# Attended sums of two units on three engines, a bias through the first layer, and an interleaved split

## The chip, the cores and the metric

The kernel runs on one core of one Trainium2 chip. The metric is the device time of one execution in microseconds, taken as the median of several runs. The core's engines are TensorE (PE in the profile), VectorE (DVE), ScalarE (ACT), GpSimd (POOL) and SyncE (SP), which here issues most of the loads. Each engine takes its own instructions in program order; semaphores order them between engines.

## What is computed

For 512 users, each with a history of 200 items of 128 features, the kernel computes attention over the history and a three-layer MLP on top. Cut to what matters (E = A = 64):

```
cand = candidate_features @ Wi + bi                  # 512 x 64
hist = history_features @ Wi + bi                    # 512 x 200 x 64
hidden = relu((cand @ Wq)[:, None, :] + hist @ Wk)
scores = where(seq < length, hidden @ Wv, -1e9)      # 512 x 200
attn = softmax(scores, axis=1)
interest = einsum('bs,bse->be', attn, hist)
avg = sum(hist * mask, axis=1) / length
x = concatenate([interest, cand, avg], axis=1)       # 512 x 192
x = relu(bn1(x @ W1 + b1)); x = relu(bn2(x @ W2 + b2)); x = relu(bn3(x @ W3 + b3))
return sigmoid(x @ Wo + bo)[:, 0]
```

`bn(x) = (x - m) / sqrt(v + eps) * g + be`.

## The kernel before, in words

**Tiling.** The users are cut in two halves of 256, which lie on partitions 0 to 63 and 64 to 127. Four users of each half are a unit (two quads of two users, 400 columns each), so there are 64 units; four units are a superblock, of which there are 16. A "pair" is one column of the tables for the MLP: one user of each half. Part 0 of the MLP takes the pairs of units 0 to 57 (232), part 1 the last 24.

**Stages of a unit.** SyncE loads 0.8 MB of history (`load`, six slots). TensorE projects it by `Wi` into `hist_ps` (`project`, L396, two passes of float32). VectorE masks it into `kept` with a running sum for the average (`masked_sum`, L539). TensorE makes the keys in `key_ps` (`keys`, L411), for the unit before. ScalarE adds the query and takes the relu (`relu`, L306). Once a superblock TensorE makes the scores (`score`, L422), VectorE the maximum (`maximum`, L561), ScalarE the exponent (`exponent`, L314), VectorE the inverse of its sum (`invert`, L567). GpSimd then normalises the weights and splits them in three bfloat16 terms (`split`, L259 to L271: `attn`, `part_a`, `rest`, `part_b`, `parts`). TensorE spreads a row of the weights over partitions (`spread_attn`, L441) for the unit seven before (`DELAY = 7`), and VectorE multiplies by `kept` and sums (`attended_sum`, L552), four instructions a unit. The history's sum lacks the bias of `Wi`, so `mean` adds it (L572, L575), and `store_interest` adds it to the attended sums (L581).

**Order.** TensorE's loop over the units is: project the first quad, project the second, scores at every fourth unit from unit 5 on, keys of the unit before, and from unit 7 on the spread of the unit seven before. The first spread waits for `parts(0)`. Warm-up matmuls on zeros (L366) stand at the start: 8, then 6, then 4 between the two quads of unit 0.

**GpSimd's queue.** Masks 0 and 1, the count, then the scale and shift of the three normalisations (L279 to L289, after the late parameters have landed), then for each superblock `split(j)` and `mask(j + 2)`. The last split is VectorE's (L626 to L635).

**The tail.** After the loop TensorE has: scores of the last superblock in two halves, keys of unit 63, the spreads of units 57, 58 and 59, stages 0 and 1 of MLP part 0, six warm-ups, the spreads of units 60 and 61, stage 2, spread 62, stage 3, spread 63, stages 0 of part 1 and 4 of part 0, then stages 1 to 4 of part 1. Stage 1 adds the interest's product to z1, which ScalarE turns into x1 (L322); x2 and x3 follow (L326, L330), and the sigmoid (L334). ScalarE loads the sigmoid's table by a one-element ACTIVATE (L354) after the last exponent. Odd units from 57 on have their spread in `key_ps`, even ones in `attn_ps`.

Of the kernel before, what the change touches and what calls it, by code (L numbers as in the profile page):

```python
# [8 lines left out]
ALU = mybir.AluOpType  # L9
ACT = mybir.ActivationFunctionType  # L10
# [21 lines left out]
DELAY = 7  # L32

SCORE_AT = SB_UNITS + 1

WARMUPS = 8
MORE_WARMUPS = 6
GAP_WARMUPS = 4
TAIL_WARMUPS = 6
COPIES = 3  # L40
# [3 lines left out]

PART_UNITS = UNITS - 6
MLP_PARTS = (slice(0, UNIT_PAIRS * PART_UNITS), slice(UNIT_PAIRS * PART_UNITS, HALF))

# [11 lines left out]
def build(nc, hist_dram, cand_dram, params_dram, lens_dram, out_dram):  # L59
    with ExitStack() as ctx:  # L60
# [49 lines left out]
        attended = sb("attended", [128, HALF])  # L110
        interest = sb("interest", [128, HALF])
        average = sb("average", [128, HALF])
# [60 lines left out]
        attn_spread = sem("attn_spread")  # L173
        attn_summed = sem("attn_summed")
        bn_steps = sem("bn_steps")
        bn_ready = sem("bn_ready")
# [3 lines left out]
        average_ready = sem("average_ready")  # L180
        interest_ready = sem("interest_ready")
        z1_ready = sem("z1_ready")
# [8 lines left out]

        block = ctx.enter_context(nc.Block())

        def wait(eng, semaphore, value):
# [25 lines left out]
        def _(pool):  # L220
# [60 lines left out]
            pool.tensor_tensor(bn_shift[:, :], param("b"), param("m"), ALU.subtract).then_inc(bn_steps, 1)  # L281
            pool.wait_ge(bn_steps, 3)
            pool.tensor_tensor(bn_scale[:, :], bn_scale[:, :], bn_power[:, :], ALU.pow).then_inc(bn_steps, 1)
            pool.wait_ge(bn_steps, 4)
            pool.tensor_tensor(bn_scale[:, :], bn_scale[:, :], param("g"), ALU.mult).then_inc(bn_steps, 1)
            pool.wait_ge(bn_steps, 5)
            pool.tensor_tensor(bn_shift[:, :], bn_shift[:, :], bn_scale[:, :], ALU.mult).then_inc(bn_steps, 1)
            pool.wait_ge(bn_steps, 6)
            pool.tensor_tensor(bn_shift[:, :], bn_shift[:, :], param("be"), ALU.add).then_inc(bn_ready, 1)  # L289

            for j in range(LAST):
                split(j)
                if j + 2 <= LAST:
                    mask(j + 2)

        @block.scalar
        def _(act):
# [39 lines left out]
            act.dma_start(params[:, 0:EARLY], params_dram[:, 0:EARLY]).then_inc(early_landed, 16)  # L337
            act.dma_start(lens_raw[:, :], lens_dram).then_inc(lens_landed, 16)
            act.wait_ge(bias_product, 1)
            act.activation(query_bias[:, :], attn_ps[:, 1, 0:1], ACT.Copy).then_inc(bias_ready, 1)  # L340
# [6 lines left out]
            for unit in range(UNITS):  # L347
                j, at = divmod(unit + 1 - SCORE_AT, SB_UNITS)
                if at == 0 and j >= 0:
                    exponent(j)  # L350
                relu(unit)
            exponent(LAST)

            act.activation(table_loader[:, :], param("bo", slice(0, 1)), ACT.Sigmoid)  # L354
            for stage in range(1, 4):
                mlp_stage(0, stage)
            mlp_stage(1, 1)
            mlp_stage(1, 2)
            mlp_stage(0, 4)
            mlp_stage(1, 3)  # L360
# [3 lines left out]
        def _(pe):  # L364
# [62 lines left out]
            def spread_attn(unit):  # L427
# [4 lines left out]
                if unit == FREE_AT:  # L432
                    pe.wait_ge(relu_done, 4 * (UNITS - 1))
                else:
                    wait(pe, attn_summed, UNIT_PAIRS * (unit - 1 if unit > FREE_AT else unit))
                banks = attn_banks(unit)
# [9 lines left out]
            def mlp_stage(n, stage):  # L446
# [9 lines left out]
                if stage == 1:  # L456
                    pe.wait_ge(interest_ready, n + 1)
                    for h in range(2):
                        rows = slice(64 * h, 64 * h + 64)
                        product = pe.matmul(z1[:, h, pairs], w1[rows, 0, :], interest[rows, pairs],  # L460
                                            start=False, stop=True, skip_group_check=True)
                    product.then_inc(z1_ready, 1)
# [22 lines left out]
            for unit in range(UNITS):  # L485
# [5 lines left out]
                if unit == 0:  # L491
                    queries()
                j, at = divmod(unit - SCORE_AT, SB_UNITS)
                if at == 0 and j >= 0:
# [6 lines left out]
                if unit >= DELAY:  # L501
                    if unit == DELAY:
                        pe.wait_ge(spread_made, 1)
                        pe.wait_ge(query_ready, 1)
                    spread_attn(unit - DELAY)

# [11 lines left out]
            for _ in range(TAIL_WARMUPS):  # L518
                keep_busy((LAST + 1) % 2)
            spread_attn(first + 3)  # L520
            spread_attn(first + 4)
            mlp_stage(0, 2)
            spread_attn(first + 5)
            mlp_stage(0, 3)
            spread_attn(first + 6)
            mlp_stage(1, 0)
            mlp_stage(0, 4)
            for stage in range(1, 5):
# [3 lines left out]
        def _(dve):  # L532
# [9 lines left out]

            def attended_sum(unit, pairs=range(UNIT_PAIRS)):
                dve.wait_ge(attn_spread, unit + 1)
                banks = attn_banks(unit)
                for c in pairs:
                    at, v = divmod(c, 2)
                    q = 2 * unit + at
                    col = UNIT_PAIRS * unit + c

                    wait(dve, attn_summed, col - 3)
                    dve.tensor_tensor_reduce(scratch[:, at, v, :], banks[:, at, v * SEQ:(v + 1) * SEQ], kept[:, q % KEPT_SLOTS, v, :],  # L552
                                             1.0, 0.0, ALU.mult, ALU.add, attended[:, col:col + 1]).then_inc(attn_summed, 1)
# [15 lines left out]
            def mean(n):  # L569
# [6 lines left out]
                                  ALU.mult).then_inc(average_ready, 1)  # L576

            def store_interest(n):
                pairs = MLP_PARTS[n]
                dve.wait_ge(attn_summed, pairs.stop)  # L580
                dve.tensor_scalar(interest[:, pairs], attended[:, pairs], param("bi"), None,  # L581
                                  ALU.add).then_inc(interest_ready, 1)

# [8 lines left out]
            for unit in range(UNITS):  # L592
# [12 lines left out]
                if unit == PART_UNITS + 2:  # L605
# [4 lines left out]

            first = UNITS - DELAY
            attended_sum(first)
            store_interest(0)
            mean(1)
            attended_sum(first + 1)
            maximum(LAST)
            attended_sum(first + 2)
            invert(LAST)
# [7 lines left out]
            dve.tensor_scalar(part_a[:, :], weights[:, bank, :], inverse, param("keep1"),  # L626
                              ALU.mult, ALU.mult).then_inc(split_steps, 1)
            dve.wait_ge(split_steps, done + 1)
            dve.scalar_tensor_tensor(out=rest[:, :], in0=weights[:, bank, :], scalar=inverse, in1=part_a[:, :],
# [6 lines left out]
            for unit in range(first + 3, UNITS):  # L636
                attended_sum(unit)
            store_interest(1)

# [60 lines left out]
```

## Time and profile before

| | |
|---|---|
| median of 3 runs | 212.09 us (210.8 to 212.43) |
| the profiled execution | 211.71 us |
| its span, first to last instruction | 209.7 us |
| TensorE (matmuls) busy | 200.9 us, 96% |
| VectorE busy | 176.8 us, 84% |
| ScalarE busy | 103.5 us, 49% |
| GpSimd busy | 62.6 us, 30% |
| mean granted clock of TensorE | 0.984 |

The busy shares are means over the span. Matmuls are pipelined and their ends are modelled, so a busy TensorE is not one at its peak. The granted clock is a share of the full 2.4 GHz. In timeline rows the second number is how long the group of instructions was busy from its start; consecutive groups of one engine can overlap a little.

### The profile page before, as it was taken

The numbers are of one execution on the slowest core, as the hardware profiler recorded it, in microseconds if no ns is written. First come the engines' busy times: TensorE is split into PE (matmuls) and PEld (weight loads), VectorE is DVE, ScalarE is ACT, GpSimd is POOL, SyncE is SP. The second block draws the span as 40 slices with busy tenths as digits, with TensorE's granted clock in tenths as the row PEclk, the third lists the DMA queues.
The fourth block names the chain that finished last, engine by engine and source line by source line (L and its number), as shares of the span: only waits on it lengthen the run. The fifth ranks groups of instructions, "written<-read, shape, count | busy, mean of one in ns | idle before, by whom it ended". The sixth has DMA issues, their size and how long they took to land.

```text
span 209.7 us, 6308 instructions
## 1 busy us (share of the span) xinstructions
PE 200.9 (96%) x2126; PEld 83.6 (40%) x2126; DVE 176.8 (84%) x1086; ACT 103.5 (49%) x302; POOL 62.6 (30%) x112
## 2 busy tenths in 40 slices
PE   7999999999999999999999999999999999997793
PEld 3422434343434434343434343343444343433422
DVE  1458578989989898989899898989898998998890
ACT  2145355545465553555453655535554536556523
POOL 7903330606051321406060513224060605131000
PEclk9999999999999999999999999999999999999985
DMA  6999999797979797987969797978879793000000
GB/s 201 398 426 416 412 419 391 245 328 249 323 245 322 237 320 266 309 307 269 321 242 300 268 323 237 316 262 317 303 253 326 238 318 130 0 0 5 3 0 0
DMA packets 10225, 53.72 MB, mean 256 GB/s; under 512 B 1105, under 2 KB 2001, under 8 KB 10194
## 3 DMA queue, kind: packets, MB, share of 16 engines
q1 hardware_dynamic: 9906, 52.95, 70.7%
q10 hardware_dynamic: 288, 0.37, 0.6%
q8 instruction: 17, 0.28, 0.5%
q14 instruction: 14, 0.11, 0.1%
HBM read 53.32 MB, written 0.00 MB: 254 GB/s over the span
## 4 chain that ended last, share of the span: by engine, by line
PE 87%; DVE 8%; ACT 2%; issue 2%; DVEq 0%; ACTq 0%
PE hist_ps L396 42%; PE key_ps L411 24%; PE score_ps L422 10%; PE attn_ps L441 5%; DVE scratch L552 3%; DVE kept L539 3%; PE score_ps L366 2%; PE score_ps L473 1%; PE score_ps L465 1%; ACT hidden L306 1%; ACT x L326 1%; PE score_ps L468 0%; PE hist_ps L411 0%; ACT result L334 0%; DVE attended L552 0%
## 5 line engine op out<-in xcount | busy, mean ns | idle before, releaser
L306 ACT ACTIVATE hidden<-key_ps,query 128x200 f32<-128x200 f32 x252 | 86.8, 427 | 54.3 <-PE key_ps L411 54.3
L396 PE MATMUL hist_ps<-history,params 128*64 128x400 f32 x512 | 100.3, 512 | 0.0
L539 DVE SCALAR_TENSOR_TENSOR kept<-item,lens,hist_ps 128x200 f32<-128x200 f32 x256 | 92.7, 419 | 7.2 <-PE hist_ps L396 7.2
L552 DVE CUSTOM_DVE_ANT_0 scratch<-attn_ps,kept 128x200 f32<-128x200 f32 x240 | 73.3, 363 | 9.2 <-PE attn_ps L441 9.2
L411 PE MATMUL key_ps<-kept,params 64*64 64x400 f32 x504 | 57.0, 521 | 0.9 <-ACT hidden L306 0.4
L396 PEld LDWEIGHTS hist_ps<-history,params 128*64 128x64 f32 x512 | 31.2, 136 | 37.1 <-issue 28.4
L259 POOL TENSOR_SCALAR attn<-weights,inv_sum 128x200 f32<-128x200 f32 x15 | 6.5, 435 | 112.6 <-DVE inv_sum L567 112.6
L411 PEld LDWEIGHTS key_ps<-kept,params 64*64 64x64 f32 x504 | 13.6, 131 | 35.9 <-issue 26.7
L422 PE MATMUL score_ps<-hidden,wv_rows 128*32 128x200 f32 x512 | 25.3, 336 | 1.2 <-ACT hidden L306 1.2
L441 PEld LDWEIGHTS attn_ps<-parts,spread 64*64 64x64 bf16 x480 | 15.7, 107 | 24.5 <-issue 19.0
L314 ACT ACTIVATE weights<-scores,neg_max 128x200 f32<-128x200 f32 x16 | 7.4, 462 | 35.5 <-DVE neg_max L561 35.5
L441 PE MATMUL attn_ps<-parts,spread 64*64 64x200 bf16 x480 | 21.5, 246 | 1.7 <-DVE parts L635 1.5
L552 DVE DVE_READ_ACCUMULATOR2_ANT attended<- 128x1 f32 x256 | 21.6, 84 | 0.0
L539 DVE DVE_READ_ACCUMULATOR kept<-item,lens,hist_ps 128x1 f32 x256 | 21.6, 84 | 0.0
L422 PEld LDWEIGHTS score_ps<-hidden,wv_rows 128*32 128x32 f32 x512 | 15.0, 109 | 14.7 <-ACT hidden L306 10.1
L251 POOL TENSOR_SCALAR mask_bias<-item,lens 128x200 f32<-128x200 f32 x16 | 15.4, 961 | 1.5
L561 DVE CUSTOM_DVE_ANT_0 scores<-score_ps,mask_bias 128x200 f32<-128x200 f32 x16 | 5.9, 366 | 4.9 <-PE score_ps L422 4.9
L264 POOL TENSOR_TENSOR rest<-attn,part_a 128x200 f32<-128x200 f32 x15 | 8.5, 569 | 1.3
L271 POOL TENSOR_TENSOR parts<-rest,part_b 128x200 bf16<-128x200 f32 x15 | 8.5, 566 | 1.3
L261 POOL TENSOR_SCALAR part_a<-weights,inv_sum,params 128x200 bf16<-128x200 f32 x15 | 7.6, 507 | 0.0
L366 PE MATMUL score_ps<-warmup 128*128 128x400 bf16 x24 | 6.4, 417 | 1.1 <-DVE warmup L584 1.1
L266 POOL TENSOR_SCALAR part_b<-rest,params 128x200 bf16<-128x200 f32 x15 | 6.5, 434 | 1.5
(69 smaller groups left out, 59.0 us busy)
## 6 DMA issues: line engine op xcount, KB each, us to landing
history<-history_dram SPq DMA_DIRECT2D x63, 800.0 KB, 5.0
history<-history_dram SPq DMA_DIRECT2D x2, 400.0 KB, 4.7
candT<-candidates_dram SPq DMA_DIRECT2D x1, 256.0 KB, 5.5
params<-parameters_dram SPq DMA_DIRECT2D x1, 248.5 KB, 12.1
params<-parameters_dram ACTq DMA_DIRECT2D x1, 226.5 KB, 2.4
lens_raw<-lengths_dram ACTq DMA_DIRECT2D x1, 136.0 KB, 3.8
probability<-result SPq DMA_DIRECT2D x1, 2.0 KB
```

The source lines that it names most:

```text
L251: pool.tensor_scalar(mask_bias[:, j % 2, :], item[:, :], row_len[:, j:j + 1], MASKED, ALU.is_ge, ALU.mult).then_inc(mask_ready, 1)
L261: pool.tensor_scalar(part_a[:, :], weights[:, bank, :], inv_sum[:, bank:bank + 1], param("keep1"), ALU.mult, ALU.mult).then_inc(split_step ...
L264: pool.tensor_tensor(rest[:, :], attn[:, :], part_a[:, :], ALU.subtract).then_inc(split_steps, 1)
L271: pool.tensor_tensor(parts[:, bank, :], rest[:, :], part_b[:, :], ALU.subtract).then_inc(parts_ready, 1)
L306: act.activation(hidden[:, g % HID_SLOTS, v, :], banks[:, v, at * SEQ:(at + 1) * SEQ], ACT.Relu, bias=query[:, 2 * g + v:2 * g + v + 1]).t ...
L366: pe.matmul(score_ps[:, bank, 0:QCOLS], warmup[:, 0:128], warmup[:, :], start=True, stop=True)
L396: product = pe.matmul(hist_ps[64 * h:64 * h + 64, g % 2, 0:QCOLS], param("wi"), history[:, slot, h, 2 * at:2 * at + 2, :].rearrange("f p s ...
L411: product = pe.matmul(banks[64 * j:64 * j + 64, h ^ j, 0:QCOLS], key_weights(h), kept[64 * h:64 * h + 64, first:first + 2, h ^ j, :], star ...
L422: product = pe.matmul(score_ps[32 * c:32 * c + 32, j % 2, 0:SEQ], wv_rows[:, c % 2, k, :], hidden[:, quad, c % 2, :], start=(k == 0), stop ...
L441: product = pe.matmul(banks[64 * h:64 * h + 64, at, v * SEQ:(v + 1) * SEQ], spread[rows, TILE_ROWS * v + 2 * k + h, :], parts[rows, j % 2, :],
L539: dve.scalar_tensor_tensor(out=kept[:, g % KEPT_SLOTS, u, :], in0=item[:, :], scalar=pair_len[:, col:col + 1], in1=hist_ps[:, g % 2, u * S ...
L552: dve.tensor_tensor_reduce(scratch[:, at, v, :], banks[:, at, v * SEQ:(v + 1) * SEQ], kept[:, q % KEPT_SLOTS, v, :], 1.0, 0.0, ALU.mult, A ...
```

## The change

- `bi` is no longer added to the attended sums (`store_interest` is gone). The product of `bi` with the first 64 rows of `W1` is made once by TensorE at unit 5, copied by ScalarE, and added by GpSimd to the first layer's shift before it is scaled.
- Units 58 and 61 (`HELPED`): the sums of the first quad stay on VectorE; for the second, ScalarE copies the spread weights from PSUM, GpSimd multiplies them by `kept`, and ScalarE sums by two accumulating copies.
- The last split on VectorE has the fourth sum of unit 59 between `part_a` and `rest`.
- Fewer warm-ups: 4, 2 and 2 instead of 6, 4 and 6. MLP part 0 has 57 units, part 1 has 7. `mean(0)` comes a unit earlier, `mean(1)` before the sums of unit 57.
- TensorE's tail: stage 2 of part 0 before the spreads of 60 and 61, stage 3 before those of 62 and 63, then stage 4. ScalarE's tail: x1 of part 0 before the table load.

Declarations of tensors and semaphores are left out:

```diff
+FOLD_AT = 5
-MORE_WARMUPS = 6
-GAP_WARMUPS = 4
-TAIL_WARMUPS = 6
+MORE_WARMUPS = 4
+GAP_WARMUPS = 2
+TAIL_WARMUPS = 2
-PART_UNITS = UNITS - 6
+HELPED = (UNITS - 6, UNITS - 3)
+
+PART_UNITS = FREE_AT
...
+        def helped_before(unit):
+            return sum(u < unit for u in HELPED)
+
+        def sums_before(unit):
+            return UNIT_PAIRS * unit - 2 * helped_before(unit)
...
             pool.wait_ge(bn_steps, 3)
+
+            pool.wait_ge(fold_ready, 1)
+            pool.tensor_tensor(bn_shift[:, 0:1], bn_shift[:, 0:1], fold_bias[:, :], ALU.add).then_inc(bn_steps, 1)
             pool.tensor_tensor(bn_scale[:, :], bn_scale[:, :], bn_power[:, :], ALU.pow).then_inc(bn_steps, 1)
-            pool.wait_ge(bn_steps, 4)
+            pool.wait_ge(bn_steps, 5)
...
             for j in range(LAST):
                 split(j)
                 if j + 2 <= LAST:
                     mask(j + 2)
+
+            for n, unit in enumerate(HELPED):
+                pool.wait_ge(help_copied, n + 1)
+
+                wait(pool, help_summed, 2 * n)
+                pool.tensor_tensor(help_product[:, :, :], help_attn[:, :, :], kept[:, (2 * unit + 1) % KEPT_SLOTS, :, :],
+                                   ALU.mult).then_inc(help_multiplied, 1)
...
+            def help_copy(n):
+                unit = HELPED[n]
+                act.wait_ge(attn_spread, unit + 1)
+
+                wait(act, help_multiplied, n)
+                act.activation(help_attn[:, :, :].rearrange("p v s -> p (v s)"), attn_banks(unit)[:, 1, 0:QCOLS],
+                               ACT.Copy).then_inc(help_copied, 1)
+
+            def help_sum(n):
+                act.wait_ge(help_multiplied, n + 1)
+                for v in range(2):
+                    col = UNIT_PAIRS * HELPED[n] + 2 + v
+                    act.activation(help_out[:, v, :], help_product[:, v, :], ACT.Copy,
+                                   accum_out=attended[:, col:col + 1]).then_inc(help_summed, 1)
...
                 relu(unit)
+                if unit == FOLD_AT:
+                    act.wait_ge(fold_product, 1)
+                    act.activation(fold_bias[:, :], attn_ps[:, 1, 0:1], ACT.Copy).then_inc(fold_ready, 1)
+            help_copy(0)
             exponent(LAST)
-
+            help_sum(0)
+
+            mlp_stage(0, 1)
             act.activation(table_loader[:, :], param("bo", slice(0, 1)), ACT.Sigmoid)
-            for stage in range(1, 4):
-                mlp_stage(0, stage)
+            mlp_stage(0, 2)
+            help_copy(1)
+            mlp_stage(0, 3)
+            help_sum(1)
+            mlp_stage(0, 4)
             mlp_stage(1, 1)
             mlp_stage(1, 2)
-            mlp_stage(0, 4)
             mlp_stage(1, 3)
             mlp_stage(1, 4)
...
-                    wait(pe, attn_summed, UNIT_PAIRS * (unit - 1 if unit > FREE_AT else unit))
+                    last = unit - 2 if unit > FREE_AT else unit - 1
+                    wait(pe, attn_summed, sums_before(last + 1))
+                    wait(pe, help_copied, helped_before(last + 1))
...
-                    pe.wait_ge(interest_ready, n + 1)
+                    pe.wait_ge(attn_summed, sums_before(pairs.stop // UNIT_PAIRS))
+                    wait(pe, help_summed, 2 * helped_before(pairs.stop // UNIT_PAIRS))
...
+                if unit == FOLD_AT:
+                    pe.wait_ge(late_landed, 16)
+                    pe.wait_ge(bias_ready, 1)
+                    pe.matmul(attn_ps[:, 1, 0:1], w1[0:EMB, 0, :], param("bi", slice(0, EMB)),
+                              start=True, stop=True).then_inc(fold_product, 1)
...
                     if unit == DELAY:
                         pe.wait_ge(spread_made, 1)
                         pe.wait_ge(query_ready, 1)
+                        pe.wait_ge(fold_ready, 1)
                     spread_attn(unit - DELAY)
...
+            mlp_stage(0, 2)
             spread_attn(first + 3)
             spread_attn(first + 4)
-            mlp_stage(0, 2)
+            mlp_stage(0, 3)
             spread_attn(first + 5)
-            mlp_stage(0, 3)
             spread_attn(first + 6)
+            mlp_stage(0, 4)
             mlp_stage(1, 0)
-            mlp_stage(0, 4)
...
             first = UNITS - DELAY
+            mean(1)
             attended_sum(first)
-            store_interest(0)
-            mean(1)
             attended_sum(first + 1)
             maximum(LAST)
-            attended_sum(first + 2)
+            attended_sum(first + 2, (0, 1, 2))
             invert(LAST)
...
+            attended_sum(first + 2, (3,))
             dve.wait_ge(split_steps, done + 1)
...
             for unit in range(first + 3, UNITS):
                 attended_sum(unit)
-            store_interest(1)
```

## Rows read from the trace of the kernel before

**Rows 1.** The page: totals (busy us, share), granted clock in 40 slices, a group.

```profile
PE 200.9 (96%) x2126; PEld 83.6 (40%) x2126; DVE 176.8 (84%) x1086; ACT 103.5 (49%) x302; POOL 62.6 (30%) x112
...
PEclk9999999999999999999999999999999999999985
...
L314 ACT ACTIVATE weights<-scores,neg_max 128x200 f32<-128x200 f32 x16 | 7.4, 462 | 35.5 <-DVE neg_max L561 35.5
```

**Rows 2.** Timeline of TensorE: projections of units 8 and 60 (start, busy us, what).

```profile
28.78 1.56 PE L396 MATMUL hist_ps<-history,params 128*64 128x400 f32 x8
...
178.49 1.56 PE L396 MATMUL hist_ps<-history,params 128*64 128x400 f32 x8
```

**Rows 3.** Timeline of GpSimd: power, last add, first and last instruction of `split(0)`.

```profile
18.73 0.89 POOL L283 TENSOR_TENSOR bn_scale<-bn_scale,bn_power 128x3 f32<-128x3 f32 x1
...
20.24 0.20 POOL L289 TENSOR_TENSOR bn_shift<-bn_shift,params 128x3 f32<-128x3 f32 x1
24.18 0.44 POOL L259 TENSOR_SCALAR attn<-weights,inv_sum 128x200 f32<-128x200 f32 x1 [3.74 <-DVE inv_sum L567]
...
26.39 0.56 POOL L271 TENSOR_TENSOR parts<-rest,part_b 128x200 bf16<-128x200 f32 x1
```

**Rows 4.** Timeline of all engines: relu of unit 5, keys of unit 6.

```profile
26.25 1.38 ACT L306 ACTIVATE hidden<-key_ps,query 128x200 f32<-128x200 f32 x4 [1.10 <-PE key_ps L411]
...
27.78 0.90 PE L411 MATMUL key_ps<-kept,params 64*64 64x400 f32 x8
```

**Rows 5.** Timeline of all engines in the tail, 193 to 205 us.

```profile
193.63 0.89 PE L422 MATMUL score_ps<-hidden,wv_rows 128*32 128x200 f32 x16 [1.16 <-ACT hidden L306]
...
195.41 0.36 DVE L561 CUSTOM_DVE_ANT_0 scores<-score_ps,mask_bias 128x200 f32<-128x200 f32 x1
...
196.39 1.28 ACT L354 ACT_TABLE_LOAD   x1
...
198.35 0.37 DVE L635 TENSOR_TENSOR parts<-rest,part_b 128x200 bf16<-128x200 f32 x1
...
198.78 0.37 PE L441 MATMUL attn_ps<-parts,spread 64*64 64x200 bf16 x8 [1.46 <-DVE parts L635]
...
199.19 0.37 DVE L552 CUSTOM_DVE_ANT_0 scratch<-attn_ps,kept 128x200 f32<-128x200 f32 x1 [0.47 <-PE attn_ps L441]
...
199.24 0.99 PE L465 MATMUL score_ps<-x,params 128*64 128x464 f32 x2
...
200.28 0.73 ACT L326 ACTIVATE x<-score_ps,bn_shift,bn_scale 64x464 f32<-64x464 f32 x1 [1.77 <-PE score_ps L465]
...
202.94 1.54 PE L473 MATMUL score_ps<-x,params 32*1 32x464 f32 x2
...
203.49 0.36 DVE L552 CUSTOM_DVE_ANT_0 scratch<-key_ps,kept 128x200 f32<-128x200 f32 x1
...
204.41 0.63 PE L460 MATMUL hist_ps<-interest,params 64*128 64x24 f32 x4
```

**Rows 6.** Windows: stretch, us, busy (x) of five engines, granted clock, DMA share, GB/s.

```profile
203.00:204.00 1.00, 1.00 (x2) 0.01 (x1) 0.96 (x8) 0.00 (x0) 0.00 (x0) 0.56 0.00 0
```

**Rows 7.** Timeline of all engines at the start, 0 to 10 us.

```profile
1.11 2.85 PE L366 MATMUL score_ps<-warmup 128*128 128x400 bf16 x8 [1.11 <-DVE warmup L584]
...
4.51 1.49 PE L366 MATMUL score_ps<-warmup 128*128 128x400 bf16 x6
...
6.75 0.85 PE L366 MATMUL score_ps<-warmup 128*128 128x400 bf16 x4
...
8.36 0.60 PE L370 MATMUL attn_ps<-params 64*128 64x1 f32 x4
...
9.00 0.17 ACT L340 ACTIVATE query_bias<-attn_ps 128x1 f32<-128x1 f32 x1 [6.10 <-PE attn_ps L370]
...
9.83 1.52 PE L396 MATMUL hist_ps<-history,params 128*64 128x400 f32 x8
```

**Rows 8.** DMA issues, the one at 2.72 us (unit 1): size, us to landing.

```profile
history<-history_dram SPq DMA_DIRECT2D x1, 800.0 KB, 6.8
```

## What the change does to the time: the prediction

> **What bounds the kernel now.** I read the totals and slices first. TensorE is busy 96% of the span and its granted clock stays at the top until the last two slices [rows 1]. So I read TensorE's own timeline: the projection of unit 8 starts at 28.78 us and that of unit 60 at 178.49 us, 149.71 us for 52 units, or 2.88 us a unit, with the same rhythm throughout [rows 2]. The engine has no idle time to give back there: whatever makes it wait once in this stretch is paid in full at the end. Then I looked at what must be ready when the stretch begins. From unit 7 on each unit also spreads an attention row (`spread_attn`), and the first spread needs `parts(0)` from GpSimd's `split(0)`. GpSimd starts that split at 24.18 and ends it at 26.39 + 0.56 = 26.95 us [rows 3]; TensorE reaches it when the keys of unit 6 end, at 27.78 + 0.90 = 28.68 us [rows 4]. The slack is 1.7 us, and that is the number to remember. Last I read the tail. There VectorE's chain sets the end: last maximum, sums, split, 16 attended sums one every 0.287 us (199.19 to 203.49 for 15 steps), the interest, then the small MLP of part 1 whose first matmul starts at 204.41 [rows 5]. The clock is already falling then: 0.56 on average over 203 to 204 us, from 2.4 towards 1.2 GHz [rows 6].
>
> **The fold, and what stands behind it.** The interest's bias now goes through the first layer. TensorE gets a two-pass matmul at unit 5. Four passes of the same shape take 0.60 us with what overlaps the next, so two cost 0.2 to 0.3; I take 0.27 us, on TensorE's path [rows 7]. ScalarE copies the product to `fold_bias` after the relu of unit 5. That relu ends at 26.25 + 1.38 = 27.63 [rows 4]; a 128x1 copy takes 0.17 us [rows 7], so `fold_ready` comes at 27.80.
>
> On GpSimd the chain that makes `bn_shift` now waits for `fold_ready`, and GpSimd runs in order: behind the waiting instruction stand the rest of that chain, all of `split(0)` and `mask(2)`. Nobody needs the scale and shift before the tail, but TensorE needs `parts(0)` at 28.68. From 27.80:
> - hand-off ACT to GpSimd: 0.06, as from `parts` (198.35 + 0.37) to TensorE (198.78) [rows 5]; 27.86
> - the new 128x1 add, at the price of the 128x3 one, 0.20 [rows 3]; 28.06
> - the power to the last add: 18.73 to 20.24 + 0.20, that is 1.71 [rows 3]; 29.77
> - `split(0)`: 24.18 to 26.95, that is 2.77 [rows 3]; 32.54
> - hand-off to TensorE 0.06; 32.60.
>
> TensorE is then idle from 28.68 to 32.60, 3.9 us. The spread's matmuls and weight loads no longer overlap the keys before them, which costs what the spread takes beyond its pitch, some 0.2 us (0.37 long, where only 0.10 stood between 28.68 and the projection's 28.78) [rows 2, 4, 5]. The delay is **4.1 us**, between 3.9 and 4.3. It can't be made up: keys, projection and scores behind it are all on TensorE, which has no gaps [rows 2]. Before, the same wait on `late_landed` was hidden, since the chain ended at 20.44, 3.7 us before `split(0)` could start [rows 3].
>
> **The clock after a hole.** No hole of this length exists in the kernel before. What rows show of the clock is this. At the start, after idleness, eight warm-up matmuls take 2.85 us (0.36 each), the next six 1.49 (0.25), the last four 0.85 (0.21) [rows 7]: the pace about doubles somewhere between 4.5 and 6 us, some 4 us after the first matmul, although the clock column gives 1.00 throughout. At the end the level falls to 1.2 GHz after a stretch of thin, interrupted matmuls [rows 6]. A hole of 3.9 us with nothing at all is thinner than that. If the clock falls, a stretch like the one at the start runs at half pace, 4 us, of which half is lost: 2.0 us at most, 0 if it doesn't fall. I take 1.7, since some of the low stretch can lie inside the hole.
>
> The Trainium skill (TensorE: Matmul & The Clock Gate, Part 1) says that the throttled state is the default, that activity releases it, and (section HAM oscillation) that a kernel whose matmul bursts stood apart by waits started every burst throttled. By it the term would be present; without it the sum would be 1.7 us less. The rows at both ends of the trace agree with the two levels, but none shows a hole in mid run.
>
> **The start.** Four warm-ups go before and between the first projections: 2 x 0.25 + 2 x 0.21 = 0.9 us of TensorE [rows 7]. But unit 1 is projected at 9.83 [rows 7], and its data land at 2.72 + 6.8 = 9.5 us [rows 8]. At most 0.3 us can come of it; I take -0.25, between -0.3 and 0. That cancels the fold's 0.27.
>
> **Moves of the two means.** `mean(0)` comes one unit earlier on VectorE, `mean(1)` before the sums of unit 57, where VectorE waits for its spread. The first is the same work at a similar place: 0, between -0.4 and +0.4. The second is part of the tail's gain.
>
> **The tail.** On VectorE the last maximum stood at 195.41 although the last scores ended at 193.63 + 0.89 = 194.52 [rows 5]: the interest, the mean and the sums of unit 58 stood in front. With the interest gone, the mean moved and two sums of unit 58 given away (0.57), the maximum follows the scores at 194.6, 0.8 us earlier; the sum between `part_a` and `rest` fills a hand-off gap, 0.1 more. `parts(15)` would end near 197.8 instead of 198.72.
>
> But ScalarE and TensorE come in between. ScalarE's copy of 400 columns (0.65, scaled from 0.73 for 464) lies under the wait for the maximum; GpSimd's product of 400 columns (0.56 for 200 and 0.20 for 3, so 0.93) as well [rows 3, 5]. The two accumulating copies, some 0.5 each as the exponent's 0.46 [rows 1], now precede the first x1, which ends near 197.3; then the second layer (0.99) stands ahead of the spread of unit 60 on TensorE and holds it until 198.3. Gain at that point 0.5 us instead of 0.9. The sigmoid's table load (1.28, and 0.1 for the small ACTIVATE behind it) now follows x1, so x2 runs 198.7 to 199.4 and the third layer, as wide as the second, to 200.4 [rows 5]; the spread of unit 62 stands behind it. The six sums of units 60 and 61 end at 200.4, the spread's data come at 200.8, and eight sums end at 203.1 to 203.2. Without an interest to store, the matmul of part 1 could start at 203.25 instead of 204.41: **-1.2 us** at best. Here the last 5.3 us are unchanged.
>
> Against it: four tail warm-ups fewer make this stretch thinner, so the clock may fall sooner. The fourth layer took 1.54 us while the clock fell, where the second, as wide, took 0.99 at 2.4 GHz [rows 5, 6]; at the low level it and `mlp_stage(1, 0)` behind it would end near 203.9 and take 0.6 of the gain, and if the third layer is slow too, another 0.6. I take **-0.8**, between -1.2 and 0. All new work of ScalarE and GpSimd for unit 61 (0.65 + 0.93 + 1.0) lies between 199.4 and 202.1 and hides under VectorE's sums; uncovered it would cost what passes 203.2.
>
> **Sum.** 4.1 + 1.7 + 0.27 - 0.25 + 0 - 0.8 = +5.0 us. The profiled execution took 211.71 us for a span of 209.7; this makes it 216.7. The median of the runs is 0.38 higher, so 217.1.
>
> **Rivals.**
> - *The hole without the clock.* Everything as above, but TensorE resumes at 2.4 GHz. For it: the clock held through gaps of 1.5 us or so late in the run [rows 1, 5]; against it: this gap is over twice as long. 212.1 + 3.3 = 215.4, or 215.0 with the whole tail gain. Chance 0.27.
> - *The hole, the clock, and a lost tail.* The low level lasts longer than at the start, or falls before the third layer in the tail, so that the gain there is nothing: 217.9 to 219. Chance 0.1.
> - *No hole: the kernel gets faster.* It needs `fold_ready` early enough, 1.77 + 2.77 + 0.2 = 4.7 us ahead of 28.68, that is by 23.9 us. From that point the new wait hides behind keys and projection, and only the tail counts: 212.1 - 0.8 = 211.3, 210.9 at best. The relu of unit 5 ends 3.7 us after that point [rows 4], so this needs an order of the queues other than the code gives. Chance 0.04.
> - *The main forecast*, 217.1, own range 216.3 to 217.9: chance 0.59.
>
> **How the numbers follow.** The low end, 214.7, lies a little below the hole without the clock and with the full tail gain (215.0), for hand-offs shorter than taken; the high end, 218.8, holds a longer low clock or the lost tail. Some 0.05 lies under it and 0.05 over it, and about as much again for terms I may have missized. About 1% (2.1 us) is what a measurement of this kernel tells from no change. Every case with the hole is above 214.2, so slower has 0.93; the case without it is within 1%, or just below where the tail gain is whole and the start adds its part: same 0.04, faster 0.03.
>
> **What would show it.** In the profile after: GpSimd's power at about 28 us instead of 18.7, with a wait for ScalarE's `fold_bias` before it; `attn` of `split(0)` near 29.8; TensorE idle 3.9 us before the first spread, with `parts` of GpSimd as releaser; a granted clock under 1.00 in the slice after it; unit 60's projection some 4 us later than 178.5 without the clock and near 184 with it. In the tail: the last maximum less than 0.2 us behind the scores, the second layer ahead of unit 60's spread, a gap on VectorE of 0.4 us before unit 62's sums. I am wrong if the first spread starts before 30 us, or if the rhythm after it is under 2.88 us a unit, so that the delay is made up.

## The result, and the profile after

The changed kernel takes 217.3 us in the median (216.96 to 218.0, 6 runs) beside 211.75 us for the kernel before (6 runs, the three known before among them). The ratio is 1.0266, with a 95% interval of 1.0242 to 1.029: slower by 2.7%. The profiled execution took 216.96 us, the shortest of the six, for a span of 214.9 us where it was 209.7 us. A few executions of the kernel before take some 2 us more than its others (214.19 us here; 213.75 to 214.11 us in later series, there at a mean granted clock of 0.975 instead of 0.984 to 0.994).

The page of the kernel after: total, the clock in 40 slices, and two groups (busy us, mean ns of one, idle time of the engine before them with what ended it). Beside [rows 1], TensorE's share fell from 96% to 94%, and there is a dip of the clock in the sixth and seventh slice, at 27 to 38 us. TensorE's spreads (L494) have lost 4.0 us waiting for GpSimd's `parts`.

```profile
PE 202.5 (94%) x2120; PEld 83.1 (39%) x2120; DVE 175.2 (82%) x1076; ACT 105.8 (49%) x313; POOL 64.5 (30%) x115
...
PEclk9999985999999999999999999999999999999985
...
L494 PE MATMUL attn_ps<-parts,spread 64*64 64x200 bf16 x480 | 21.5, 248 | 4.0 <-POOL parts L289 4.0
```

The timeline of all engines around it, where [rows 3] and [rows 4] stood in the kernel before. Read it from the top: the relu of unit 5, ScalarE's copy, GpSimd's add after 9.10 us of waiting, the power, the last add, `split(0)` from 30.09 to 32.85, and only then the spread, after 4.01 us in which TensorE did nothing.

```profile
26.55 1.38 ACT L334 ACTIVATE hidden<-key_ps,query 128x200 f32<-128x200 f32 x4 [1.10 <-PE key_ps L462]
...
27.81 0.19 ACT L397 ACTIVATE fold_bias<-attn_ps 128x1 f32<-128x1 f32 x1
...
28.08 0.90 PE L462 MATMUL key_ps<-kept,params 64*64 64x400 f32 x8
28.14 0.19 POOL L303 TENSOR_TENSOR bn_shift<-bn_shift,fold_bias 128x1 f32<-128x1 f32 x1 [9.10 <-ACT fold_bias L397]
28.28 0.89 POOL L304 TENSOR_TENSOR bn_scale<-bn_scale,bn_power 128x3 f32<-128x3 f32 x1
...
29.80 0.20 POOL L310 TENSOR_TENSOR bn_shift<-bn_shift,params 128x3 f32<-128x3 f32 x1
30.09 0.43 POOL L277 TENSOR_SCALAR attn<-weights,inv_sum 128x200 f32<-128x200 f32 x1
...
32.29 0.56 POOL L289 TENSOR_TENSOR parts<-rest,part_b 128x200 bf16<-128x200 f32 x1
...
32.99 0.55 PE L494 MATMUL attn_ps<-parts,spread 64*64 64x200 bf16 x8 [4.01 <-POOL parts L289]
33.47 0.29 PEld L447 LDWEIGHTS hist_ps<-history,params 128*64 128x64 f32 x4 [0.29 <-issue]
```

The windows of the same stretch (us, busy us of PE, PEld, DVE, ACT and POOL with counts, granted clock, DMA share, GB/s). TensorE does nothing from 30 to 32; the clock goes to 0.50, that is 1.2 GHz, inside that stretch (near 30.8 by the mean of 0.69) and comes back between 36 and 38.

```profile
28.00:30.00 2.00, 0.90 (x8) 0.24 (x8) 0.83 (x6) 0.96 (x4) 1.62 (x5) 1.00 1.03 422
30.00:32.00 2.00, 0.00 (x0) 0.00 (x0) 0.00 (x0) 0.42 (x2) 1.72 (x4) 0.69 1.02 413
32.00:34.00 2.00, 1.00 (x10) 0.51 (x12) 0.41 (x3) 0.00 (x0) 1.74 (x3) 0.50 0.28 115
34.00:36.00 2.00, 2.00 (x8) 0.47 (x4) 1.59 (x10) 0.00 (x0) 0.00 (x0) 0.50 0.04 8
36.00:38.00 2.00, 2.00 (x20) 0.68 (x19) 0.78 (x4) 0.08 (x1) 0.00 (x0) 0.60 0.35 61
38.00:40.00 2.00, 2.00 (x28) 0.87 (x28) 1.94 (x13) 1.30 (x4) 0.00 (x0) 1.00 0.84 339
```

The starts of the projections in TensorE's timelines show how the 5.2 us come together. "Before" and "after" are the two profiled executions; the last column is the difference to the row above. Of the -0.18 between units 9 and 60, 0.12 comes of a single unit: in the kernel before, unit 50 took 2.63 us, and 2.51 after.

| start of | before | after | later by | what was added |
|---|---|---|---|---|
| unit 1 | 9.83 | 9.96 | 0.13 | the start: +0.13 |
| unit 6 | 23.62 | 23.91 | 0.29 | the fold's matmul: +0.16 |
| unit 7 | 26.12 | 26.43 | 0.31 | +0.02 |
| unit 8 | 28.78 | 33.47 | 4.69 | the hole: +4.38 |
| unit 9 | 31.28 | 37.94 | 6.66 | the low clock: +1.97 |
| unit 60 | 178.49 | 184.97 | 6.48 | -0.18 |
| unit 63 | 187.91 | 194.54 | 6.63 | the mean's move: +0.15 |
| end of the span | 209.7 | 214.9 | 5.2 | the tail: -1.43 |

The tail after, beside [rows 5]. The last maximum follows the scores (200.26 + 0.89) by 0.1 us instead of 0.9; the second layer (203.69) stands ahead of the spread of unit 60; VectorE waits 0.29 us for unit 62's spread; there is no interest to store, so part 1's matmul on the attended sums (209.60) follows the last sum.

```profile
200.26 0.89 PE L473 MATMUL score_ps<-hidden,wv_rows 128*32 128x200 f32 x16 [1.16 <-ACT hidden L334]
...
201.22 0.37 DVE L624 CUSTOM_DVE_ANT_0 scores<-score_ps,mask_bias 128x200 f32<-128x200 f32 x1 [0.43 <-PE score_ps L473]
...
203.69 0.98 PE L519 MATMUL score_ps<-x,params 128*64 128x456 f32 x2 [0.45 <-ACT x L350]
204.03 0.37 DVE L692 TENSOR_TENSOR parts<-rest,part_b 128x200 bf16<-128x200 f32 x1
204.60 0.14 PEld L494 LDWEIGHTS attn_ps<-parts,spread 64*64 64x64 bf16 x8 [0.72 <-DVE parts L692]
...
207.12 0.37 DVE L615 CUSTOM_DVE_ANT_0 scratch<-attn_ps,kept 128x200 f32<-128x200 f32 x1 [0.29 <-PE attn_ps L494]
...
209.13 0.36 DVE L615 CUSTOM_DVE_ANT_0 scratch<-key_ps,kept 128x200 f32<-128x200 f32 x1
...
209.60 0.61 PE L514 MATMUL hist_ps<-attended,params 64*128 64x28 f32 x4
```

### The profile page after: what moved, and what is told of

Read it like the earlier page. It is cut to its first block, busy times and chain, and to the rows that moved or that the text cites. A ratio compares the mean times of both kernels' runs of the same rounds, so it can differ in the third digit from the quotient of the medians.

```text
span 214.9 us, 6310 instructions
## 1 busy us (share of the span) xinstructions
PE 202.5 (94%) x2120; PEld 83.1 (39%) x2120; DVE 175.2 (82%) x1076; ACT 105.8 (49%) x313; POOL 64.5 (30%) x115
## 4 chain that ended last, share of the span: by engine, by line
PE 87%; ACT 4%; DVE 4%; POOL 2%; issue 2%; DVEq 0%; ACTq 0%; POOLq 0%
PE hist_ps L447 42%; PE key_ps L462 23%; PE score_ps L473 11%; PE attn_ps L494 4%; PE score_ps L417 2%; DVE kept L599 2%; DVE scratch L615 1%; ACT hidden L334 1%; PE score_ps L527 1%; PE score_ps L522 1%; ACT x L350 1%; ACT x L358 1%; ACT L403 1%; ACT x L354 0%; PE hist_ps L507 0%
## 5 line engine op out<-in xcount | busy, mean ns | idle before, releaser
L447 PE MATMUL hist_ps<-history,params 128*64 128x400 f32 x512 | 102.1, 520 | 0.5 <-DVE kept L599 0.5
L494 PEld LDWEIGHTS attn_ps<-parts,spread 64*64 64x64 bf16 x480 | 15.4, 108 | 28.1 <-issue 24.1
L494 PE MATMUL attn_ps<-parts,spread 64*64 64x200 bf16 x480 | 21.5, 248 | 4.0 <-POOL parts L289 4.0
L417 PE MATMUL score_ps<-warmup 128*128 128x400 bf16 x16 | 5.4, 487 | 1.1 <-DVE warmup L641 1.1
```

Source lines behind the costliest of these rows:

```text
L417: pe.matmul(score_ps[:, bank, 0:QCOLS], warmup[:, 0:128], warmup[:, :], start=True, stop=True)
L447: product = pe.matmul(hist_ps[64 * h:64 * h + 64, g % 2, 0:QCOLS], param("wi"), history[:, slot, h, 2 * at:2 * at + 2, :].rearrange("f p s ...
L494: product = pe.matmul(banks[64 * h:64 * h + 64, at, v * SEQ:(v + 1) * SEQ], spread[rows, TILE_ROWS * v + 2 * k + h, :], parts[rows, j % 2, :],
```

## The experiments

**The theory**: the wait for `fold_bias` stands in GpSimd's queue ahead of `split(0)`, so TensorE has a hole before the first spread, and the hole costs the clock. **The rivals**: the clock falls because there are fewer warm-ups; the new tail costs the time; the loss is a fixed one that doesn't hang on when the fold comes.

**The wait and the five instructions that it holds back moved, nothing else.** `chain_later`:

```diff
+            def scale_and_shift():
+                pool.wait_ge(fold_ready, 1)
+                pool.tensor_tensor(bn_shift[:, 0:1], bn_shift[:, 0:1], fold_bias[:, :], ALU.add).then_inc(bn_steps, 1)
...
+                pool.tensor_tensor(bn_shift[:, :], bn_shift[:, :], param("be"), ALU.add).then_inc(bn_ready, 1)
...
             for j in range(LAST):
                 split(j)
                 if j + 2 <= LAST:
                     mask(j + 2)
+                if j == 0:
+                    scale_and_shift()
```

> The changed kernel, with GpSimd's wait for the folded bias and the chain behind it moved after split(0) and mask(2). If that wait's place in GpSimd's queue makes the loss, the hole of 4.4 us before the first spread and the 2.0 us of low clock behind it both go: 217.3 - 6.4 = 210.9 us, a ratio of 0.996 to the kernel before, and TensorE's granted clock stays at 1.00 until the tail. If the clock falls because there are fewer warm-ups, only the hole goes: 212.9. If the new tail is what costs the time, it stays near 217.

Measured: 210.41 us, ratio 0.9929 (0.9909 to 0.9948). Again on another chip (`chain_later_again`):

> The same kernel as chain_later, on this chip beside the next and the last one: 210.4 us, 0.993 of the kernel before.

Measured: 210.35 us, 0.9938 (0.9917 to 0.9959). One move in one queue turns 2.7% slower into 0.6 to 0.7% faster. The medians fall by 6.9 us where 6.4 were expected; between the profiled executions it is 6.4 (216.96 and 210.58), from which the 6.4 had been read. The timeline of `chain_later`: `split(0)` ends at 26.93 + 0.56, the chain runs behind `mask(2)`, and unit 8 is projected at 29.26.

```profile
26.93 0.56 POOL L289 TENSOR_TENSOR parts<-rest,part_b 128x200 bf16<-128x200 f32 x1
27.59 0.97 POOL L269 TENSOR_SCALAR mask_bias<-item,lens 128x200 f32<-128x200 f32 x1
28.64 0.19 POOL L304 TENSOR_TENSOR bn_shift<-bn_shift,fold_bias 128x1 f32<-128x1 f32 x1
...
28.95 0.38 PE L497 MATMUL attn_ps<-parts,spread 64*64 64x200 bf16 x8
29.26 1.56 PE L450 MATMUL hist_ps<-history,params 128*64 128x400 f32 x8
```

**The hole kept, the clock kept.** `fill_hole` has TensorE run warm-ups in the hole:

```diff
                         pe.wait_ge(fold_ready, 1)
+                        for _ in range(20):
+                            keep_busy()
```

> The changed kernel with the hole kept, but 20 warm-up matmuls (0.17 us each, 3.3 us) issued by TensorE in front of the first spread. If the low clock comes from the empty stretch, it stays at 1.00 and the 2.0 us go, while the hole's 4.4 us stay: 217.3 - 2.0 = 215.3 us, ratio 1.017. If the clock falls for another reason: 217.3. If the added matmuls are a load of their own: above 217.3.

Measured: 214.94 us (4 runs), 1.0142 (1.0113 to 1.0171). Its windows have the clock at 1.00 all through, with the spread at 33.04, as late as in the changed kernel, and the pace agrees: unit 8 is projected at 33.34 and unit 9 at 35.84, 2.50 us later.

```profile
30.00:32.00 2.00, 2.00 (x14) 1.14 (x12) 0.00 (x0) 0.55 (x2) 1.72 (x5) 1.00 1.01 416
32.00:34.00 2.00, 1.56 (x16) 0.61 (x16) 0.54 (x3) 0.00 (x0) 1.82 (x3) 1.00 0.48 195
```

So the empty stretch lowers the clock, and the warm-ups left out elsewhere don't. By the medians the two parts of the loss are 2.4 us (clock) and 4.5 us (hole, against `chain_later`).

**The fold one unit earlier, one unit later.** `FOLD_AT` is 4 and 6.

> The changed kernel with the fold one unit earlier (FOLD_AT 4). The copy then follows the relu of unit 4, which ends near 25.4, so GpSimd's chain starts near 25.7, split(0) near 27.6 and ends near 30.4: TensorE idles 1.5 us instead of 4.0. If the clock holds through that: 217.3 - 2.5 - 2.0 = 212.8 us. If any hole at this place costs the clock: 214.8. If the loss doesn't come from this wait: 217.3.

> The changed kernel with the fold one unit later (FOLD_AT 6). The copy follows the relu of unit 6, so it comes near 30.6, 2.6 us later, and so does the first spread: TensorE idles some 6.6 us. By the queue's order the time is 217.3 + 2.6 = 219.9 us, with about the same low clock behind the hole (1.5 to 2.3 us). If the loss is a fixed one it stays 217.3.

Measured for 4: 212.32 us, 1.0023 (0.9999 to 1.0048). For 6, one run: 218.35 us, where 219.9 was expected. TensorE's timeline of `fold_at_4` (start, busy us, and in brackets the idle time before with its releaser):

```profile
28.75 0.90 PE L462 MATMUL key_ps<-kept,params 64*64 64x400 f32 x8
31.18 0.37 PE L494 MATMUL attn_ps<-parts,spread 64*64 64x200 bf16 x8 [1.53 <-POOL parts L289]
31.47 2.87 PE L447 MATMUL hist_ps<-history,params 128*64 128x400 f32 x8
```

and that of `fold_at_6`:

```profile
28.08 0.90 PE L462 MATMUL key_ps<-kept,params 64*64 64x400 f32 x8
35.51 0.55 PE L494 MATMUL attn_ps<-parts,spread 64*64 64x200 bf16 x8 [6.52 <-POOL parts L289]
35.98 2.75 PE L447 MATMUL hist_ps<-history,params 128*64 128x400 f32 x8
```

The hole follows the fold: 1.53, 4.01 and 6.52 us, where the queue's order gave 1.5, 3.9 and 6.6.

The clock doesn't follow in proportion. In `fold_at_6` the windows of two us have it at 0.90 from 30 to 32, 0.50 until 38 and 0.89 from 38 to 40, so it fell near 31.6 and was back near 38.4; only 2.9 us of that had work, so at half pace some 1.5 us were lost, the low end of what I had put. The unit behind the hole shows 1.2 of it (35.98 to 39.67, 3.69 us instead of 2.50), the spread 0.2 (0.55 us instead of 0.37). Against the changed kernel's profile its span is 1.4 us longer (216.3): 2.5 for the hole, less 0.8 for the clock behind it, less 0.3 in the last microseconds, where its clock was higher. I had left both deductions out.

In `fold_at_4` the ten executions lie in two groups, eight from 211.8 to 212.8 and two at 214.4 and 215.1. The profile is of the one at 215.1: the projection behind its hole of 1.53 us took 2.87 us instead of 1.56, and unit 9 came 4.14 us behind unit 8 (31.47 to 35.61) instead of 2.50. So in this execution a hole of 1.53 us was followed by the low clock, at a price of 1.6 us. The eight others fit the case in which the clock holds (212.8 expected), but no trace of one is at hand. Nor is the hole shown to be the cause: the kernel before has its longer executions without one, though its 17 beside `fold_at_4` lie between 211.23 and 212.61 us.

**The fold alone**, on the kernel before, in the place of the change and then behind `mask(2)`; the old tail, all warm-ups, nothing helped, `mlp_stage` 1 reads `attended` and `store_interest` is gone:

> The kernel before with the fold alone (the matmul at unit 5, ScalarE's copy, GpSimd's wait and add in the place where the change has them, no interest stored), all warm-ups, no helped units, the old tail. If the fold's place makes the whole loss, this one is slower than the changed kernel, which has the tail's gain: 211.9 + 0.15 + 4.4 + 2.0 less some 0.3 for the interest = 218.2 us. If fewer warm-ups had a part in the low clock, it keeps a granted clock of 1.00 and takes 216.2.

> As fold_alone (the old tail, all warm-ups, nothing helped), with GpSimd's wait and chain behind split(0) and mask(2). It shows what the folded bias gives without the hole: 0.3 us on VectorE for part 0 and some 0.2 for part 1, less 0.15 for the matmul at unit 5, so 211.5 us or 0.997 to 0.998. If the tail's gain of the change (1.5 us) came with the fold rather than with the new orders, it would be near 210.4.

Measured: 217.51 us, 1.0266 (1.0234 to 1.0297), and 211.01 us, 0.9973 (0.9948 to 0.9998). The fold in that place makes the whole loss, with all warm-ups: TensorE idles 4.01 us and the clock falls. 211.01 us is 0.5 below the 211.5 expected, and the interval ends just below 1. In `fold_alone` the clock stayed low for less time than in the changed kernel (0.93, 0.50 and 0.72 over 32 to 38 us, some 3.4 us in all, against some 6.8 us), and the unit behind the hole took 4.10 us (33.76 to 37.86) instead of 2.5: 1.6 lost where I had put 2.0. I had this kernel 0.7 us too high (218.2 us), and its profile of 217.48 us shows the terms: the clock 1.6 for 2.0, the hole 4.2 for 4.4 (its spread ran at the full pace, 0.37 us), the kernel before 211.7 for 211.9, the stretch from unit 63 to the end 0.8 us shorter than before, for 0.3, and against these a start that was 0.6 us later (unit 1 at 10.45). TensorE's timeline of `fold_alone`:

```profile
33.47 0.37 PE L450 MATMUL attn_ps<-parts,spread 64*64 64x200 bf16 x8 [4.01 <-POOL parts L274]
33.76 2.94 PE L405 MATMUL hist_ps<-history,params 128*64 128x400 f32 x8
36.63 1.13 PE L420 MATMUL key_ps<-kept,params 64*64 64x400 f32 x8
37.59 0.34 PE L450 MATMUL attn_ps<-parts,spread 64*64 64x200 bf16 x8
```

**The other parts, on top of `chain_later`.** Warm-ups at the start back to 6 and 4, warm-ups in the tail back to 6, and `HELPED = ()` with its calls on ScalarE removed:

> As chain_later (210.4 us), with the start's warm-ups of the kernel before (6 and 4 instead of 4 and 2). My prediction said that leaving them out gives 0.25 us: then this takes 210.65. The trace of the changed kernel has the projection of unit 1 0.13 us later than before and its first projection slower (1.33 us for four matmuls, not 0.89): if that is the rule, this takes 210.3.

> As chain_later (210.4 us), with 6 warm-ups in the tail instead of 2. They take 0.7 us more of TensorE, which waits there for x1 for 0.45 us: if the clock is the same, 210.4 to 210.7. If four warm-ups fewer let the clock fall sooner in the tail and slow the fourth layer and the first matmuls of part 1, this is faster, 209.9 to 210.3.

> As chain_later (210.4 us), but no unit is helped: VectorE makes all four sums of units 58 and 61. Two sums of 0.287 us come back ahead of the last maximum and two more behind the last split, 1.15 us. Less the 0.3 us in which VectorE waits in the changed kernel for the spread of unit 62: 210.4 + 0.85 = 211.2 us. If ScalarE's and GpSimd's new work was itself on the path, it is less, down to 210.4.

Measured: 210.88 us, 0.9957 (0.9938 to 0.9977); 210.92 us, 0.9942 (0.9916 to 0.9968); 210.7 us, 0.9946 (0.9923 to 0.9969). `chain_later` itself had 0.9929 and 0.9938, so none of the three stands clear of it: what each is worth is 0.6 us at most by the middle values, and not settled by the times. The timelines say more, though each is of one execution. From the projection of unit 63 to part 1's matmul on the attended sums (the last that goes into z1) it takes, in us:

| kernel | unit 63 | z1 of part 1 | between |
|---|---|---|---|
| before | 187.91 | 204.41 | 16.50 |
| `fold_alone_later` | 187.72 | 203.71 | 15.99 |
| `later_no_help` | 188.20 | 203.40 | 15.20 |
| `later_old_tail_warmups` | 188.13 | 203.15 | 15.02 |
| `chain_later` | 188.56 | 203.57 | 15.01 |
| after | 194.54 | 209.60 | 15.06 |

Of the tail's gain of 1.5 us, 0.5 came with the interest that isn't stored, 0.8 with the new orders (the moved means and the smaller part 0 among them, not taken apart), and 0.2 with the help of ScalarE and GpSimd. The 0.5 is in part the clock: in the kernel before the interest ended at 203.90 + 0.24 = 204.14, and the matmul still stood until 204.41 behind the fourth layer, which took 1.54 us there and 0.93 in `fold_alone_later`. Two instructions fewer on VectorE before the last maximum gave next to nothing, since the maximum then waits for the scores: even with both of them, in `later_no_help`, it stands at 194.93, 0.13 us behind the scores' end, in the timeline of all engines:

```profile
193.92 0.88 PE L472 MATMUL score_ps<-hidden,wv_rows 128*32 128x200 f32 x16 [1.16 <-ACT hidden L337]
...
194.93 0.36 DVE L623 CUSTOM_DVE_ANT_0 scores<-score_ps,mask_bias 128x200 f32<-128x200 f32 x1
```

**Where the mean may stand.** `mean(0)` at unit 59 costs TensorE 0.5 us at unit 61. TensorE's timeline of `chain_later` has the wait:

```profile
182.06 1.56 PE L450 MATMUL hist_ps<-history,params 128*64 128x400 f32 x8 [0.51 <-DVE kept L602]
```

and with the mean at unit 56 the timeline of `later_mean_at_56` has another, through the maximum and the exponent:

```profile
173.01 0.36 DVE L627 CUSTOM_DVE_ANT_0 scores<-score_ps,mask_bias 128x200 f32<-128x200 f32 x1
...
173.41 0.46 ACT L345 ACTIVATE weights<-scores,neg_max 128x200 f32<-128x200 f32 x1 [2.53 <-DVE neg_max L627]
...
175.37 0.90 PE L465 MATMUL key_ps<-kept,params 64*64 64x400 f32 x8 [0.29 <-DVE kept L602]
```

> As chain_later, with mean(0) at the end of unit 56 on VectorE instead of unit 59. In the traces with it at unit 59, its 0.8 us come in a row of units where VectorE is 0.4 us behind TensorE, and the projection of unit 61 waits 0.5 us for VectorE. At the end of unit 56 VectorE next meets the maximum of a score unit, before and behind which it idles 0.4 and 0.6 us. If those gaps take it up, this gives 0.5 us against chain_later: 0.990 to 0.991 of the kernel before, about 209.9 us. If a move of the mean is worth nothing, it is the same as chain_later.

> As chain_later, with mean(0) on VectorE in unit 57 between the maximum and the attended sums. later_mean_at_56 gained nothing: there the mean delayed the maximum by 0.4 us, with it ScalarE's exponent and relu, and TensorE's keys waited 0.3 us. Behind the maximum the mean's 0.8 us fall in the 0.6 us in which VectorE waits for the spread, and 0.2 us of delay are less than the 0.4 us by which VectorE is ahead of what TensorE needs. If that reading is right, no unit from 57 to 62 takes more than 2.5 us (4.0 with scores), and the time is 0.4 us under chain_later: 209.9 to 210.0, 0.991 to 0.992 of the kernel before. If every place costs the same, it is 210.4, 0.994.

Measured: 210.23 us, 0.9939 (0.9921 to 0.9957), no gain over `chain_later`; and 209.99 us, 0.9924 (0.9898 to 0.995). At unit 56 the mean delays the maximum, the exponent behind it, the relu and so the keys: unit 58 takes 2.86 us (173.52 to 176.38) instead of 2.5. At unit 57, behind the maximum, the projections start at 170.10, 174.09, 176.61, 179.11, 181.60 and 185.60: the rhythm is undisturbed, so in the trace the mean has become free. As a time this is within the noise of `chain_later`; in the profiled executions 0.35 us of the gain went again at the end, where the clock fell sooner (5.4 us from part 1's matmul at 203.12 to the end of the span, 5.0 in `chain_later`). It has the lowest median of all kernels here; that it beats `chain_later` isn't shown, that it beats the kernel before is.

## Why the prediction was right, and where its terms were off

The forecast was 217.1 us and the measured 217.3. The mechanism was right: the wait ahead of `split(0)`, TensorE's idle time, the low clock behind it. That the figure lies within 0.2 us is in part luck. In the profiles the loss is 5.2 us, for 5.0, by errors that cancelled: hole +0.3, clock +0.3, start +0.4, tail -0.6, the others under 0.2. Of these four only the clock is within its own bounds. And between the medians it is 5.6 us: the forecast was added to 212.09 us, the median of three runs, where six gave 211.75.

- **The hole.** By the sum `parts(0)` was to be ready at 32.54 and the first spread at 32.60 in the time of the kernel before. It came at 32.99, with 0.3 us of it from what stood ahead. Idle time 4.01 us for 3.9; delay of unit 8's projection 4.38 for 4.1. Of the missing 0.3, 0.1 is idle time: the hand-offs took longer (0.14 us from ScalarE's copy to GpSimd and again from `parts` to TensorE, where 0.06 stood), less 0.1 because the copy overlapped the end of the relu. The other 0.2 is the spread at the low clock, 0.48 us to the projection behind it, where at the full pace (`fold_alone`) it is 0.29. The hole's cause is shown by the move of the wait, by the shift of the fold both ways and by the fold alone.
- **The clock.** Term 1.7, measured 1.97 in the profile and 2.4 between the medians of the changed kernel and `fill_hole`. The upper bound of 2.0, drawn from the length of the low stretch at the start, was too tight by the medians: the low stretch lasted some 6.8 us here and 4.6 us of it had work. That it falls had chance 0.69 in my cases; it fell in each of the three profiles with an empty hole of 4 us or more. The rule of the Trainium skill (TensorE: Matmul & The Clock Gate, section HAM oscillation), that every burst behind such a wait starts throttled, fits the changed kernel: the window from 32 to 34 us has a granted clock of 0.50. In `fold_alone` the clock was low just behind the burst's start: the spread still ran at the full pace (0.37 us), and the level fell near 33.7, 0.25 us later.
- **The start.** Term -0.25, measured +0.13. The step that failed is the price of a warm-up taken from a mean over a stretch in which the clock rose. In the changed kernel the pace was still low when the first projection came (four matmuls in 1.33 us, not 0.89), and the time saved was lost in it. Where the pace rose early (`later_old_tail_warmups`, four warm-ups in 0.85 us), TensorE waited 0.72 us for the load of unit 0's second half instead, and unit 1 came at 9.79. Over the traces unit 1 starts at 9.45 to 10.45 in the four kernels with the old warm-ups (`fold_alone_later`, `later_old_start`, before, `fold_alone`) and at 9.62 to 10.60 in the ten with the new ones (`later_mean_at_56` first, `fold_at_4` last, which waits for its load), so the traces show no gain in it. The times leave up to 0.6 us open (`later_old_start` 0.9957 beside 0.9929 and 0.9938).
- **The fold's matmul.** Term 0.27, measured 0.16 between units 1 and 6.
- **The mean.** Term 0, measured +0.15, the difference of two costs that I hadn't seen in the kernel before: 0.42 us at unit 60 there (units 62 to 63 take 2.92 us, 184.99 to 187.91) and 0.57 at unit 59.
- **The tail.** Term -0.8, bounds -1.2 and 0, measured -1.43. Maximum 0.82 us and `parts` 0.95 us earlier against the projection of unit 63, for 0.8 and 0.9. Then ScalarE's two accumulating copies took 0.79 us, not 1.0 (202.09 to 202.88), so x1 and the second layer came sooner and held the spread of unit 60 by 0.1 and not 0.5 us. The last sum starts 0.99 us earlier and the matmul behind it 1.44: before, it also stood behind the interest and behind the fourth layer (1.54 us with the clock falling, here 1.12).
- **The clock in the tail.** The clock did fall 1.5 us sooner in relation to the work (0.64 over 208 to 209 us), but it met only the end of the fourth layer and stage 0 of part 1, for which nobody waited then; six warm-ups instead of two change nothing (15.02 and 15.01 us). With two warm-ups it fell 13.7 us behind the projection of unit 63 here and 16.4 us behind it in `chain_later` (near 205.0), with six 14.0 us behind it in `later_old_tail_warmups` (near 202.1), so the number of warm-ups is not what sets it.
- **The sums given away.** The two of unit 58 I credited with 0.57; they brought the last maximum forward by 0.06 (it starts 6.67 us behind the projection of unit 63 in `chain_later`, 6.73 in `later_no_help`), and the move of interest and mean alone lets the maximum meet the scores.

The low bound of the range came from the case without the low clock: 215.4 forecast, 214.94 measured with `fill_hole`. The other side, no hole, was put at 211.3, or 210.9 at best; with the wait moved it is 210.4.

## What to carry to other kernels

Before a wait is put into an engine's queue, list everything that stands behind it there and when each of it is due: here the wait belonged to a chain needed some 170 us later, and behind it stood `split(0)`, whose result was due 0.9 us after the wait could end. A hole of 4 us or more in TensorE's stream in mid run was paid twice here, as the hole and as matmuls at 1.2 GHz behind it. Work given away by an engine brings only what the next thing it waits for allows; look which wait ends last at the place where the work was.

## What the runs showed of the hardware

- The clock's price isn't tied to the hole's length. Holes of 4.01 us were followed by low stretches of some 6.8 us (changed kernel) and 3.4 us (`fold_alone`), a hole of 6.52 us by one of 6.8 us that began inside it, and a hole of 1.53 us by one of 3.4 us in the one execution profiled (`fold_at_4`). The two long ones began inside the hole (near 30.8 and 31.6 us), the two short ones behind its end (near 33.7, and near 31.6 in `fold_at_4`, where the hole ended at 31.18). That is an order seen in four traces; why the same hole of 4.01 us gave one of each stays open.
- Twenty matmuls on zeros, 128x128 by 400 columns, in the hole held the clock at 1.00 (`fill_hole`), and the spread behind them came no later (33.04 us, 32.99 without them).
- A GpSimd instruction with two tensor operands took 1.04 us for 400 columns and 0.56 for 200; ScalarE's accumulating copy of 200 columns took 0.35 us with 0.19 us for the accumulator, the next one starting 0.35 us after it.
